# Selective scan on one core: TensorE's side work regrouped over pairs of items

## The reference, cut to what matters

```
dA = exp(dt_t[..., None] * A);  dBx = dt_t[..., None] * B_t[:, None, :] * x_t[..., None]
h = dA * h + dBx                      # along the tokens, for each channel and state
y = einsum('bdn,bn->bd', h, C_t)      # sum over the 16 states
y = (ys + D * xc) * silu(z)           # z: the gate, a projection of the input
return einsum('bdl,hd->blh', y, out_proj_w)
```

## Time and profile before

| what | value |
|---|---|
| median of 3 runs | 5343.03 us (5336.1 to 5351.6) |
| the profiled execution | 5348.99 us |
| its span | 5346.8 us |
| mean granted clock of PE | 0.956 |
| busy share PE, DVE, POOL, ACT | 90%, 58%, 41%, 37% |
| scan stage, first DVE scan to last | about 2395 to 4241 us |

### The profile page before, as it was taken

How to read it: one execution, slowest core, us unless ns; L and a number is a source line. 1 busy time by engine, 2 the same in 40 slices (tenths; PEclk the granted TensorE clock), 3 DMA queues, 4 the chain that set the end, 5 groups by cost and what they waited for, 6 DMA issues and landing times. The chain is left out here.

```text
span 5346.8 us, 50880 instructions
## 1 busy us (share of the span) xinstructions
PE 4819.9 (90%) x19376; PEld 2730.1 (51%) x19376; DVE 3122.5 (58%) x3354; ACT 2004.1 (37%) x2937; POOL 2172.7 (41%) x1187
## 2 busy tenths in 40 slices
PE   8997989989868899968788998999899899999998
PEld 4443234467636444425556665666566544457443
DVE  1673468755457323238999898889889622103522
ACT  1454520045322111126666666656666410002100
POOL 1003430000022100019999898999889642100421
PEclk8899999999989999989999999999999999999999
DMA  2001030000010112142115446434644420000001
GB/s 75 1 1 67 22 128 24 28 16 1 9 34 1 35 64 71 55 112 59 36 42 164 127 136 172 144 117 136 181 127 136 138 78 0 24 0 28 20 16 47
DMA packets 177487, 357.30 MB, mean 67 GB/s; under 512 B 21278, under 2 KB 56222, under 8 KB 173150
## 3 DMA queue, kind: packets, MB, share of 16 engines
q1 hardware_dynamic: 169182, 326.26, 20.1%
q0 software_dynamic: 8064, 27.80, 1.4%
HBM read 296.31 MB, written 57.67 MB: 66 GB/s over the span
## 5 line engine op out<-in xcount | busy, mean ns | idle before, releaser
L3019 POOL TENSOR_TENSOR l2scan_h<-l2scan_dtx,l2scan_Bb 128x1024 f32<-128x1024 f32 x384 | 902.4, 2365 | 66.8 <-PE l2scan_yT L2785 54.6
L2785 PE MATMUL l2scan_yT<-ident,l2scan_h 128*128 128x128 f32 x4096 | 547.5, 282 | 153.5 <-POOL l2scan_h L3044 145.7
L2785 PEld LDWEIGHTS l2scan_yT<-ident,l2scan_h 128*128 128x128 f32 x4096 | 484.2, 145 | 360.5 <-POOL l2scan_h L3044 202.2
L2967 ACT ACTIVATE l2scan_ring<-l2scan_dt,l2scan_A 128x512 f32<-128x512 f32 x768 | 506.7, 683 | 410.9 <-DVE l2scan_h L3091 259.6
L3044 POOL TENSOR_TENSOR l2scan_h<-l2scan_h,l2scan_Cb 128x1024 f32<-128x1024 f32 x256 | 604.6, 2362 | 51.5 <-DVE l2scan_h L3091 41.3
L2767 PE MATMUL l2scan_big<-state,l2scan_Wz 128*128 128x512 f32 x1024 | 475.8, 597 | 0.8 <-ACT l2scan_zs L2923 0.8
L2411 PE MATMUL l2in_acc<-state,l2in_W 128*128 128x512 f32 x1024 | 445.0, 595 | 10.4 <-DMA l2in_W<-l_attn_in_x 10.4
L2536 PE MATMUL l2scan_big<-l2scan_oy,l2scan_oW 128*128 128x512 f32 x768 | 359.3, 598 | 9.7 <-DMA l2scan_oy<-l_y 9.3
L2411 PEld LDWEIGHTS l2in_acc<-state,l2in_W 128*128 128x128 f32 x1024 | 194.4, 190 | 258.7 <-issue 247.5
L3102 DVE TENSOR_TENSOR l2scan_h<-l2scan_ring,l2scan_Cb 128x1024 f32<-128x1024 f32 (+1 forms) x307 | 315.5, 1042 | 4.4
L3091 DVE TENSOR_TENSOR_SCAN l2scan_ring<-l2scan_ring,l2scan_carry,l2scan_h 128x512 f32<-128x512 f32 x256 | 312.9, 1268 | 5.9 <-ACT l2scan_ring L2967 5.9
(11 more groups left out here) (426 smaller groups left out, 8490.1 us busy)
## 6 DMA issues: line engine op xcount, KB each, us to landing
l2scan_oy<-l_y SPq DMA_DIRECT2D x192, 512.0 KB
l2scan_Wz<-l_attn_in_z SPq DMA_DIRECT2D x64, 512.0 KB, 3.5
l2scan_oW<-l_attn_out_w SPq DMA_DIRECT2D x192, 128.0 KB
l_xc<-l2in_xc SPq DMA_DIRECT2D x16, 1024.0 KB, 4.8
l2scan_xc<-l_xc SPq DMA_DIRECT2D x64, 256.0 KB, 4.8
l2scan_Cb<-l_bc SPq DMA_DIRECT2D x128, 128.0 KB, 6.4
l_y<-l2scan_zs SPq DMA_DIRECT2D x64, 256.0 KB, 3.6
l2scan_Bb<-l_bc SPq DMA_DIRECT2D x96, 128.0 KB, 5.1
```

What stands on the lines that cost most here:

```text
L2785: last = t.matmul(yT[:, k, :], h[:, st % SLOTS, j, k * P:(k + 1) * P], K.ident[:, :], is_transpose=True, start=g == 0 and j == 0 and k == ...
L2967: a.activation(bank(st, j) if maker(st) == "P" else h[:, st % SLOTS, j, :], dt[:, q % 2, :], ACT.Exp, scale=A[:, ct, n:n + 1]).then_inc(dA ...
L3019: g_.tensor_tensor(h[:, st % SLOTS], dtx[:, None, :].to_broadcast([P, SGR, NT]), Bb[:, rows_at(g), :], ALU.mult).then_inc(dBx_ok, 1)
```

## The change

The same instructions are issued; none is added or removed. Their order changes on four queues. PE: z of the even item stands in s16 1, 2, 3, out in s16 5 to 10 with 1, 2, 1, 2, 1, 1 pieces, z of the odd item in s16 13, 14, 15, none of it in the next item. That is 16 products in each item. ACT: the gate of the odd item is made in step 1 of the next, behind `keep_dtx` and ahead of `keep`; the gate of the even item in step 5. DVE: the tile is added in step 4 of the odd item, behind `pre_dt`, instead of step 5. SP: six pieces stand ahead of the store and two behind it.

```diff
-    SHARE = (1, 1, 2, 1, 1, 2)
+    SHARE = (1, 2, 1, 2, 1, 1)
@@ block.sync
-                        late = range(at + 5, at + PIECES)
+                        late = range(at + 6, at + PIECES)
-                        for n in range(at + 3, at + 5):
+                        for n in range(at + 3, at + 6):
                             proj.load(e, n)
@@ block.tensor
-                    if s16 == 0 and q:
-                        z_part(q - 1, 6, KT)
-                    if st == 6 or q and s16 == 2:
+                    if st == 6 or q and s16 == 1:
                         z_part(q, 0, 2)
-                    if st == 7 or q and s16 == 3:
+                    if st == 7 or q and s16 == 2:
                         z_part(q, 2, 5)
                     if st == 8:
                         z_part(0, 5, KT)
-                    if q and s16 == 4:
+                    if q and s16 == 3:
                         z_part(q, 5, KT)
+                    if s16 == 13:
+                        z_part(q, 0, 3)
                     if s16 == 14:
-                        z_part(q, 0, 2)
+                        z_part(q, 3, 5)
                     if s16 == 15:
-                        z_part(q, 2, 6)
-                    if 6 <= s16 < 12 and q >= CT:
-                        out_part(q - q % 2, s16 - 6)
+                        z_part(q, 5, KT)
+                    if 5 <= s16 < 11 and q >= CT:
+                        out_part(q - q % 2, s16 - 5)
                 total(STEPS - 2)
                 total(STEPS - 1)
-                z_part(ITEMS - 1, 6, KT)
                 turn_back(ITEMS - 1)
@@ block.scalar
                         if ct == 0:
                             diagonals(c, 0)
+                        if q % 2 == 0:
+                            gate(q - 1)
                     if g == 2 and q:
                         keep(q - 1)
-                        if q % 2 == 0:
-                            gate(q - 1)
-                    if g == 6 and q and q % 2 == 0:
+                    if g == 5 and q and q % 2 == 0:
                         gate(q)
@@ block.vector
-                    if g == 5 and q >= CT and q % 2 == 1:
+                    if g == 4 and q >= CT and q % 2 == 1:
                         proj.add(v, (q - CT) // 2)
```

## The result

The changed kernel takes 5356.81 us (median of 19 runs, 5347.26 to 5364.14), the one before 5347.85 in 19 runs beside them: ratio 1.002, 95% interval 1.0014 to 1.0027. It is 0.2% slower, which the interval tells from zero, but within the 0.3% that the forecast calls no change; the forecast was 5344 with 5300 to 5382. The profiled execution took 5356.0 us, against 5348.99.

What follows compares the result with a forecast made beforehand. A loop through several nearly full engines, 57.00 us per pair, was taken as the bound. Terms -1 + 6 - 2 - 2 = +1 gave 5350 against the profiled 5348.99, median 5344, range 5300 to 5382.

Steps and rivals of the forecast that it cites:

- the loop that would close: Chunks 1 to 3: through PE's `turn_dtx` and ACT's odd gate to step 2's scan, 56.94 us against 57.00.
- The loads of the ring: Output pieces' DMA: nothing added; a slightly late last piece is covered by PE's 1.3 us wait for the add.
- The wait for `spread`: DVE's 2.51 us wait in step 13 of the odd item goes, as `spread` comes 3.4 us earlier.
- the add: Step 4 of the odd item on DVE: PE waits some 1.3 us for it ahead of z in s16 13.
- Steady pairs: Pairs of chunks 1 to 3 away from chunk ends: 21 x 0.06 = -1 us, bounds -54 and +37.
- Chunk 0: Its 7 pairs: later `turn_dtx` and gate ahead of step 2 cost about 0.9 a pair, +6 us, bounds 0 and +25.
- Chunk ends: First pairs of chunks 2 and 3 gain 2 us each by earlier `Wdt`, chunk 1's loses 2: taken -2.
- Last item: Last odd item: `spread` comes 2 us earlier while the last gate waits for the last `total` anyway: -2 us.
- A: Rival: the gate does not close the loop; 54.4 us per pair, 5291, half of it 5317; chance whole or half 0.26.
- B: Rival: PE's stretch before `turn_dtx`, s16 13 to 15, catches a wait; +40 us, 5383; chance 0.28.
- C: Rival: DVE and POOL take the stall's place, another loop of 57, same time; chance 0.46 together with the forecast.
- The drain: ACT's table loads: about 1.38 us more each would give a period of 59.7, +57 us; left out of the sum.

Runs made afterwards that it cites:

- e1: The changed kernel with a plain copy in place of silu and no table loads around it: 5304.53 us, ratio 0.9919 to the kernel before.
- e3: The kernel before with only SHARE = (1, 2, 1, 2, 1, 1), three output pieces in the even item, five in the odd: 5369.85 us, ratio 1.0046.
- e12: The kernel before with SHARE = (1, 2, 1, 2, 1, 1) and four instead of five pieces ahead of the store on SP: 5320.22 us, ratio 0.9943.
- e11: The kernel before with SHARE (1, 2, 1, 1, 1, 1, 1), four pieces ahead of the store, and `Wdt` loaded ahead of B and C rows: 5267.89 us, ratio 0.9853.

## Why the prediction was right

**The mechanism.** The forecast named the loop that would close and its size, 56.94 per pair. Links from start to start around a loop add up to the period whatever they are, so the sum is no evidence; each link against its forecast is. In the pair shown they give 57.6: `pre_dt` to `dtx` 0.77, to `total` of step 7 13.07, to `total` of step 8 7.29 (forecast 6.94), to `pre_dt` 7.09, to z 1.44 (1.35), to the next pair's `turn_dtx`, at 3139.90, 12.23 (12.15), to the scan of step 2 5.28 (5.22), to `pre_dt` 10.41 (10.39). Every link is within 0.1 but one: the piece of s16 9 starts 1.10 behind `dt_tile` (3116.22 to 3117.32) instead of 0.86, and `total` stands 1.82 behind it instead of 1.72; PEld waits 0.91 for that piece's DMA. The loads of the ring are not free, as I had said, since it is not the last piece but the one before it that comes late, ahead of `total` of step 8, where no wait covers it. Over the steady pairs of chunks 1 to 3 this link takes 6.9 to 8.3 us, where before it took 6.94 in all but one. No run changes this alone.

**PE's side.** The wait for `spread` went; PE waits 1.37 for the add (1.3 forecast), and 28.9 us in 21 stretches in all. Two waits were not foreseen: 0.81 for the gate at z, and 1.17 for `keep` at `total` of step 0, which the early gate also delays. PE's slack before step 7 covered both, and they used it up: PE waited 1.80 there before and does not wait at 3111.85 now, 0.05 behind the end of POOL's product (3109.42 + 2.38). So a second chain is as long as the forecast one, and the forecast did not have it: from ACT's gate through `keep` and PE's own queue to `total` of step 7.

**The sum, term by term**, over the two profiled executions, from the starts of the pairs. Steady pairs: forecast -1 for 21; six pairs in each of chunks 1, 2 and 3 give +3.4, +5.0 and +5.2, in all +13.6 for 18. This is the mis-sized term, 0.75 a pair instead of -0.06, and its sign was wrong within its stated bounds. Chunk 0: forecast +6, measured +2.7 over six pairs; in one of them the low clock came at 2648.30 (granted clock 0.50, 1.00 before in the same stretch), but only two of the even items were longer by more than 1 us. Chunk ends: -2 forecast; -2.3 and -2.5 for the two with the `Wdt` wait, -1.0 for the first, and +2.0 in the very first pair, not foreseen. Last item: -2, measured -2.2. Together +10 in the stage; the rest of the program was 3 us shorter, which two executions can differ by. So there is some luck in the total: +7 was measured and +1 forecast, but the steady pairs alone were 14.6 us off, and the other terms and that rest took some 8.5 of it back.

**The rivals.** A (the gate does not close the loop) is what e1 comes near to: 55.4 per pair, ratio 0.992, against 54.4 worked out. The table loads are what its condition fails by, but its price of 2.6 us a pair was too high: 1.6 came, and then PE with its wait for the add is the bound. B's place, PE's stretch before `turn_dtx`, stayed without an extra wait in chunks 1 to 3: it took 12.23. C (DVE and POOL take the stall's place) is not what the waits show: in chunks 1 to 3 DVE's wait for `low` went only from 56.8 to 62.8 us, that for ACT ahead of the scans into `ring` from 13.5 to 52.1. The drain that the Trainium skill, ScalarE: Activation LUTs, What ACT_TABLE_LOAD costs, adds to each load does not show: the exponential starts 1.30 behind the start of the second load of 1.28, and the period stayed under the 59.7 that it would give.

## What to carry to other kernels

When engines run one loop in step, count not only each engine's share but the length of every closed chain through them: here 3.4 us taken out of one chain were worth nothing as long as a gate with two table loads stood ahead of the exponentials that the next scan needs. Moving an instruction earlier for one consumer makes all that stand behind it in its queue later for the others, as on ACT here; and a load that has to wait does the same to those behind it in the DMA queue, as in e3. The version that won moved single pieces off the chain that was critical, had `Wdt` loaded earlier, and left the gate where it was.

## What the runs showed of the hardware

The order of the DMA queue mattered as much as that of the engines: one load of `Wdt` behind a piece whose buffer came free late turned a gain of 0.6% (e12) into a loss of 0.5% (e3). And three engines can be nearly full at once: in e11 PE is busy 99%, DVE 96% and POOL 95% of a stretch of 325 us.
